# A gated delta-rule layer with a feed-forward layer on one core: the preamble shares one SBUF layout with the head units

## The reference, cut to what matters

```python
# x: (4, 1024, 256); 16 key heads, 32 value heads of 128, chunks
x = x + layernorm(attn(layernorm(x)))
x = x + layernorm(ffn(layernorm(x)))       # weights are lut[idx]; silu(gate) * up, down

def attn(x):
    mixed = silu(causal_conv4(x @ W_qkv.T))              # q, k, v
    z, b, a = x @ W_z.T, x @ W_b.T, x @ W_a.T
    beta = sigmoid(b)
    g = -exp(A_log) * softplus(a + dt_bias)              # then cumulated inside each chunk
    # per head and chunk: decay = exp(gc_i - gc_j) below the diagonal,
    # T = (I + strict(beta * k k' * decay))^-1, and a state carried from chunk to chunk
    S_new = S * exp(g_last) + (k * exp(g_last - g)).T @ v_new
    core = (q * exp(g)) @ S + ((q @ k.T) * decay) @ v_new
    return (rmsnorm(core) * norm_w * silu(z)) @ W_out.T
```

## Time and profile before

| | |
|---|---|
| median of 3 runs | 4870.68 us (4868.75 to 4873.02) |
| the profiled execution, its own time | 4866.2 us |
| its span, first to last instruction | 4864.0 us |
| PE busy in the span | 4643.0 us (95%) |
| DVE, ACT, POOL busy | 3760.0, 2864.6, 2725.4 us |
| granted TensorE clock, mean | 0.980 of full speed |

### The profile page before, as it was taken

How to read it: one execution, slowest core, us unless ns; L and a number is a source line. 1 busy time by engine, 2 the same in 40 slices (tenths; PEclk the granted TensorE clock), 3 DMA queues, 4 the chain that set the end, 5 groups by cost and what they waited for, 6 DMA issues and landing times. The chain is left out here.

```text
span 4864.0 us, 98703 instructions
## 1 busy us (share of the span) xinstructions
PE 4643.0 (95%) x33236; PEld 3450.4 (71%) x33236; DVE 3760.0 (77%) x8539; ACT 2864.6 (59%) x5549; POOL 2725.4 (56%) x8582
## 2 busy tenths in 40 slices
...
DMA packets 579249, 219.43 MB, mean 45 GB/s; under 512 B 455212, under 2 KB 541612, under 8 KB 577080
## 3 DMA queue, kind: packets, MB, share of 16 engines
...
## 5 line engine op out<-in xcount | busy, mean ns | idle before, releaser
L718 DVE SCALAR_TENSOR_TENSOR CV<-pp,CW,CV 128x1023 f32<-128x1023 f32 (+2 forms) x768 | 980.6, 1277 | 115.0 <-ACT CV L1002 108.0
L428 PE MATMUL pp<-xnT,W 128*128 128x512 f32 x2048 | 977.1, 601 | 40.6 <-DMA W<-wqkv 30.8
L1222 POOL TENSOR_TENSOR TM<-UL,XL 128x126 f32<-128x126 f32 (+22 forms) x1984 | 701.7, 354 | 277.8 <-issue 140.5
L1225 POOL TENSOR_TENSOR UL<-UL,TM 128x126 f32<-128x126 f32 (+22 forms) x1984 | 734.5, 370 | 155.4
L428 PEld LDWEIGHTS pp<-xnT,W 128*128 128x128 f32 x2048 | 375.9, 194 | 313.4 <-issue 268.3
L1086 ACT ACTIVATE QE<-qa,TAB 128x128 f32<-128x128 f32 x1024 | 319.8, 364 | 457.5 <-PE qa L553 455.8
L595 PE MATMUL emit<-Wz,xnT 128*128 128x256 f32 x2048 | 505.1, 389 | 1.0 <-DVE OACC L892 1.0
L616 PE MATMUL emit<-Wo,NTr 128*128 128x256 f32 x2048 | 497.8, 386 | 3.1 <-ACT NTr L1131 1.4
L1283 POOL TENSOR_TENSOR wd<-wd,wv 128x268 f32<-128x268 f32 x240 | 224.3, 934 | 475.3 <-DVE wv L903 475.3
L1097 ACT ACTIVATE VS<-qa,EB 128x128 f32<-128x128 f32 x1024 | 320.2, 366 | 234.6 <-PE qa L563 225.9
L827 DVE SCALAR_TENSOR_TENSOR R<-kv,TAB,V 128x128 f32<-128x128 f32 x1024 | 310.1, 344 | 182.4 <-PE kv L543 177.8
...
## 6 DMA issues: line engine op xcount, KB each, us to landing
W<-wqkv SPq DMA_DIRECT2D x256, 128.0 KB, 2.9
XL<-xb SPq DMA_DIRECT2D x128, 256.0 KB, 3.9
...
xb<-X SPq DMA_DIRECT2D x512, 32.0 KB, 1.6
...
ub<-UL SPq DMA_DIRECT2D x128, 128.0 KB, 3.0
N<-ub SPq DMA_DIRECT2D x256, 64.0 KB, 2.2
...
```

Source lines behind the costliest of these rows:

```text
L428: ins = t.matmul(bk.pp[:, 512 * h:512 * h + 512], m.W[:, c, k, :], m.xnT[:, w // KH % 2, c, 512 * h:512 * h + 512], start=c == 0, stop=c == 1)
L718: v.scalar_tensor_tensor(m.CV[:, t, d:S], bk.pp[:, 0:S - d], m.CW[:, w % KH, t, 3 - d:4 - d], m.CV[:, t, d:S], ALU.mult, ALU.add).then_inc ...
L1222: p.tensor_tensor(m.TM[:, 0:a, 0:b], m.UL[:, 0:a, k:k + 1].to_broadcast([128, a, b]), m.XL[:, k, k + 1:32].unsqueeze(1).to_broadcast([128, ...
L1225: p.tensor_tensor(m.UL[:, 0:a, k + 1:32], m.UL[:, 0:a, k + 1:32], m.TM[:, 0:a, 0:b], ALU.subtract).then_inc(s["sub"], 1)
```

## The change: what it does

1. The preamble's tensors become views of unit tiles that are not yet used (`p.X` is AT and N1, `p.xnT` is xnT and OACC, `p.tabs` are XL, Wz, Wo and half of V). The four `pre_` functions go; each engine has a `start` ahead of the only remaining barrier and a `loop` behind it.
2. `start` normalises the first 8 tiles by themselves, then the other 24. Tile 0 of unit 0 is projected between the two; the gate rows come next, with 32 weight columns for each sequence written to its own 32 PSUM partitions; then tiles 1 and 2 of unit 0, its transposes, `kred(0)`, `nk(0)` and `ldg(0)`. The normalised rows of sequences 0 and 1 stay in SBUF.
3. The pieces' DMAs of sequences 1 to 3 (six) are issued by POOL, after `nk(0)` and before the barrier.
4. `tables` (transposes into columns, Exp, negation) stands behind the barrier, and POOL issues four DMAs for them, one for each kind. Loads into XL, Wz, Wo, TAB and the copies into V (`xl`, `ldz`, `ldo`, `ldt`, `vev(0)`) wait for `tabw`, which these four DMAs raise.
5. The warm-up steps are written out once, without the parts done in `start`; from step 0 on, the loop bodies have the order of before.
6. `newton` takes three steps in place of four, everywhere.

```diff
-    for i in range(4):
+    for i in range(3):
...
-def pre_sp(nc, s, g, p, dr):
...
-def pre_dve(nc, s, g, p, bk):
...
-def pre_pe(nc, s, g, p, bk):
...
-def pre_act(nc, s, g, p, bk):
...
+def main_sp(nc, s, g, m, p, dr):
...
+    def start():
+        q.dma_start(p.X[0], dr.x.rearrange("(n p) h -> p n h", p=128)[:, 0:8, :]).then_inc(s["x0"], 16)
+        q.dma_start(g.cf[:], dr.c_f32[:, 0:129]).then_inc(s["cf"], 16)
+        ldw(0, 0)
+        ldw(0, 1)
+        q.dma_start(m.CW[:], dr.convw.rearrange("k p t j -> p k t j")).then_inc(s["cwl"], 16)
+        for j in range(1, 4):
+            q.dma_start(p.X[j], dr.x.rearrange("(n p) h -> p n h", p=128)[:, 8 * j:8 * j + 8, :]).then_inc(s[f"x{j}"], 16)
+        q.dma_start(p.wb, dr.wba).then_inc(s["wb"], 16)
+        ldw(0, 2)
+        ldw(0, 3)
+        q.dma_start(p.hd[:, 0:1], dr.dtb).then_inc(s["hd"], 16)
+        q.dma_start(p.hd[:, 1:2], dr.alog).then_inc(s["al"], 16)
+        q.dma_start(p.reset, dr.c_reset).then_inc(s["reset"], 16)
+        q.dma_start(p.last127, dr.c_f32[:, 129:257]).then_inc(s["l127"], 16)
+        q.dma_start(g.mask, dr.c_mask).then_inc(s["cb"], 16)
+        sp.wait_ge(s["ini"], 1)
+        q.dma_start(m.GR[:].bitcast(I32), dr.c_gr).then_inc(s["cbh"], 16)
+        q.dma_start(m.nw[:], dr.normw).then_inc(s["nwl"], 16)
+        q.dma_start(m.lc[:], dr.lut.to_broadcast([128, LUT])).then_inc(s["lcl"], 16)
+        for b in range(2, NB):
+            sp.wait_ge(s["xt0"], 4 * b + 4)
+            q.dma_start(dr.xnd[b], p.xnT[b]).then_inc(s["xnw"], 16)
+        for k, d in enumerate((dr.gcd, dr.gad)):
+            sp.wait_ge(s["pieces"], 5 * k + 5)
+            q.dma_start(d[:, :, 0:S], p.pieces[k][0:32]).then_inc(s["g3a"], 16)
+        for sem, n in (("cb", 16), ("cbh", 16), ("lcl", 16), ("nws", 1), ("xnw", 32)):
+            sp.wait_ge(s[sem], n)
+        ldg(0)
+    def loop():
+        ldx(0)
...
+def main_pe(nc, s, g, m, p, bk):
...
+    def start():
+        pe.wait_ge(s["cf"], 16)
+        banks = (bk.out, bk.ml, bk.mr, bk.kv)
...
+        tx(0)
+        pe.wait_ge(s["xt0"], 4)
+        for h in range(2):
+            pj(0, 0, h)
+        for b in range(1, NB):
+            tx(b)
+        pe.wait_ge(s["wb"], 16)
+        pe.wait_ge(s["xt0"], NT // 2)
+        rows = (bk.ml, bk.mr, bk.kv, bk.qa)
+        for part in range(2):
+            for half in range(2):
+                for b in range(NB):
+                    for h in range(2):
+                        ins = t.matmul(rows[2 * part + half][32 * b:32 * b + 32, :], p.wb[:, h, part, :],
+                                       p.xnT[b][:, h, 512 * half:512 * half + 512], start=h == 0, stop=h == 1)
+                ins.then_inc(s["rowp"], 1)
+        for h in range(2):
+            pj(0, 1, h)
+        for h in range(2):
+            tpq(0, h)
+        for h in range(2):
+            tpk(0, h)
+        for h in range(2):
+            pj(0, 2, h)
+    def tables():
+        banks = (bk.out, bk.ml, bk.mr, bk.kv)
+        for k, (row, ready) in enumerate(((p.ra, "gst"), (p.rb, "bst"))):
+            pe.wait_ge(s[ready], 5 if k == 0 else 3)
+            pe.wait_ge(s["rows"], 4)
+            for h in range(2):
+                pb = banks[2 * k + h]
+                for n in range(4):
+                    c = 4 * h + n
+                    ins = t.transpose(pb[:, n * 128:(n + 1) * 128], row[:, c * 128:(c + 1) * 128], g.ident)
+                ins.then_inc(s["colp"], 1)
+        pe.wait_ge(s["l127"], 16)
+        pe.wait_ge(s["col"], 2)
+        for h, pb in enumerate((bk.qa, bk.out)):
+            t.matmul(pb[:, :], p.last127, p.GC[:, 16 * h:16 * h + 16, :], start=True, stop=True).then_inc(s["glp"], 1)
+    def loop():
+        tables()
+        decp(0, 0)
+        kq(0, 0)
...
+    def start():
+        def stats(j, n0, n1):
+            for n in range(n0, n1):
+                dv.wait_ge(s[f"x{n // 8}"], 16)
+                v.bn_stats(p.st[:, n, :], p.X[n // 8][:, n % 8, :]).then_inc(s["bs"], 1)
+            for n in range(n0, n1):
+                dv.wait_ge(s["bs"], n + 1)
+                v.bn_aggr(p.mv[:, n, :], p.st[:, n, :]).then_inc(s["mv"], 1)
+            dv.wait_ge(s["mv"], n1)
+            v.tensor_scalar(p.var[:, n0:n1], p.mv[:, n0:n1, 1], 1e-5, None, ALU.add).then_inc(s["rsq"], 1)
+            newton(dv, s["rsq"], 14 * j + 1, p.var[:, n0:n1], p.rstd[:, n0:n1], p.tn[:, n0:n1])
+            dv.wait_ge(s["rsq"], 14 * j + 14)
+            for n in range(n0, n1):
+                v.tensor_scalar(p.X[n // 8][:, n % 8, :], p.X[n // 8][:, n % 8, :], p.mv[:, n, 0:1], p.rstd[:, n:n + 1],
+                                ALU.subtract, ALU.mult).then_inc(s["xn"], 1)
...
+        v.memset(m.GL[:], 1.0).then_inc(s["ini"], 1)
+        v.memset(m.VL[:], 0.0)
+        stats(0, 0, 8)
+        dv.wait_ge(s["cwl"], 16)
+        stats(1, 8, NT)
+        for d in range(1, 4):
+            cvk(0, 0, d)
+        dv.wait_ge(s["nwl"], 16)
...
+        dv.wait_ge(s["hd"], 16)
+        v.tensor_scalar(p.ra, p.ra, p.hd[:, 0:1], None, ALU.add).then_inc(s["gst"], 1)
+        dv.wait_ge(s["gst"], 1)
+        v.scalar_tensor_tensor(p.rc, p.ra, -1.0, p.ra, ALU.mult, ALU.max).then_inc(s["gst"], 1)
+        for d in range(1, 4):
+            cvk(0, 1, d)
+        dv.wait_ge(s["bexp"], 2)
+        v.scalar_tensor_tensor(p.rb, p.rb, 0.0, p.rd, ALU.min, ALU.subtract).then_inc(s["bst"], 1)
+        dv.wait_ge(s["aexp"], 2)
+        v.scalar_tensor_tensor(p.rc, p.ra, 0.0, p.rc, ALU.max, ALU.add).then_inc(s["gst"], 1)
...
+            dv.wait_ge(s["pieces"], n + 4)
+            v.tensor_copy(pc[:, 2, :], p.rc).then_inc(s["pieces"], 1)
+        kred(0)
+    def tables():
+        dv.wait_ge(s["col"], 4)
+        for h, pb in enumerate((bk.qa, bk.out)):
+            dv.wait_ge(s["glp"], h + 1)
+            v.tensor_tensor(p.DL[:, 16 * h:16 * h + 16, :], pb[:].rearrange("p (t h) -> p t h", h=32),
+                            p.BT[:, 16 * h:16 * h + 16, :], ALU.add).then_inc(s["dl"], 1)
+        dv.wait_ge(s["egt"], 4)
+        v.tensor_scalar(tab(p, NEG), tab(p, EG), -1.0, None, ALU.mult).then_inc(s["dtab"], 1)
+    def loop():
+        tables()
+        mk(0, 0)
+        x(0, 0)
...
+        if w == 0:
+            ac.wait_ge(s["tabw"], 64)
+        elif w == 1:
+            ac.wait_ge(s["g3w"], 96)
...
+        xt(0)
+        ac.wait_ge(s["cwl"], 16)
+        cv0(0, 0)
+        for b in range(1, NB):
+            xt(b)
+        ac.wait_ge(s["al"], 16)
+        a.activation(p.hd[:, 2:3], p.hd[:, 1:2], ACT.Exp).then_inc(s["ea"], 1)
+        for i, (part, row) in enumerate(((0, p.rb), (1, p.ra))):
+            for half in range(2):
+                ac.wait_ge(s["rowp"], 2 * i + half + 1)
+                a.activation(row[:, half * 512:half * 512 + 512], rows[2 * part + half][:, :],
+                             ACT.Copy).then_inc(s["rows"], 1)
+        ac.wait_ge(s["bst"], 1)
+        a.activation(p.rd, p.rd, ACT.Exp, scale=-1.0).then_inc(s["bexp"], 1)
+        cv0(0, 1)
+        ac.wait_ge(s["gst"], 2)
+        a.activation(p.rc, p.rc, ACT.Exp, scale=-1.0).then_inc(s["aexp"], 1)
+        ac.wait_ge(s["bexp"], 1)
+        a.activation(p.rd, p.rd, ACT.Ln, bias=1.0).then_inc(s["bexp"], 1)
+        ac.wait_ge(s["aexp"], 1)
+        a.activation(p.rc, p.rc, ACT.Ln, bias=1.0).then_inc(s["aexp"], 1)
+        qt(0)
+        kt(0)
+        for h in range(2):
+            qsq(0, h)
+        for h in range(2):
+            kev(0, h)
+        ksq(0)
+    def tables():
+        banks = (bk.out, bk.ml, bk.mr, bk.kv)
+        for k, col in enumerate((p.GC, p.BT)):
+            for h in range(2):
+                ac.wait_ge(s["colp"], 2 * k + h + 1)
+                a.activation(col.rearrange("p (b c) h -> p c b h", b=NB)[:, 4 * h:4 * h + 4],
+                             banks[2 * k + h][:].rearrange("p (c b h) -> p c b h", c=4, b=NB),
+                             ACT.Copy).then_inc(s["col"], 1)
+        ac.wait_ge(s["col"], 2)
+        a.activation(tab(p, EG), cols(p.GC), ACT.Exp).then_inc(s["egt"], 1)
+        for h, pb in enumerate((bk.qa, bk.out)):
+            ac.wait_ge(s["dl"], h + 1)
+            a.activation(tab(p, EGLS, h), cols(pb[:].rearrange("p (t h) -> p t h", h=32)),
+                         ACT.Exp).then_inc(s["egt"], 1)
+        a.activation(tab(p, EGLB), cols(p.DL), ACT.Exp).then_inc(s["egt"], 1)
+    def loop():
+        tables()
...
+    def start():
+        po.wait_ge(s["xtp"], NT // 2)
+        gp.memset(m.N1[0][:], 0.0)
+        gp.memset(m.N1[1][:], 0.0)
+        nk(0)
+        for k, d in enumerate((dr.gcd, dr.gad)):
+            po.wait_ge(s["pieces"], 5 * k + 5)
+            for b in range(1, NB):
+                gp.dma_start(d[:, :, b * S:b * S + S], p.pieces[k][32 * b:32 * b + 32]).then_inc(s["g3w"], 16)
+    def tables():
+        po.wait_ge(s["egt"], 4)
+        po.wait_ge(s["dtab"], 1)
+        for k in range(4):
+            gp.dma_start(dr.tabd[:, :, k].rearrange("k p t r -> p k (t r)"),
```

(69 more changed lines are left out.)

1024 lines of the change are left out of this document (499 added, 525 removed).

## The result

| | median us | runs |
|---|---|---|
| before | 4871.23 | 4868.75 to 4873.02, 4 |
| after | 4811.42 | 4805.85 to 4813.38, 4 |

The ratio of after to before is 0.9875 [0.9863, 0.9886]: the changed kernel is faster by 59.8 us, where 42.7 were forecast (4828, range 4812 to 4852). The profiled execution of after took 4813.38 us with a span of 4811.3, and 52.8 less than that of before.

What follows compares the result with a forecast made beforehand. TensorE is busy in 95% of the span, so only changes where it waits matter. The mark's 35.5 us plus 7.2 in feed-forward make 42.7; 4866.2 less that is 4823.5, with 4.5 added 4828, range 4812 to 4852.

Steps and rivals of the forecast that it cites:

- The gate rows: In the preamble, neighbouring sequences' products on separate output partitions overlap by one record: 20.8 us of rows instead of 27.7.
- rival 2: Gate rows in the preamble overlap fully, all four sequences at once: 6.9 us of rows, kernel 4814 us; chance 0.05.
- Statistics and chain: Preamble: first data at 6.7 us, eight tiles done at 15.7, all at 36.4; last piece at 83.4.
- The POOL DMAs: Six DMAs of the pieces ahead of the barrier, 0.95 us each, 5.7 in all; barrier opens at 95.8.
- Behind the barrier: Transposes, products, Exps and negation take 11.1 us to the first mask at 106.9; att of (0,3) at 126.1.
- the mark: Time at which x(0,3) of unit 0 is done: 126.1 instead of 161.65, 35.5 us earlier, moving the end alike.
- the signs that the prediction named for being wrong: vt(0) moving less than the att of (0,3), or a changed length of the stretch between unit 0 and last unit.
- Rival 3: POOL's table DMAs behind the barrier are slow, deciding from 16 us a table; 4886 us at 20; whole case 0.09.
- Rival 4: After unit 0, vt(0) doesn't follow the mark: 4838 to 4845 us; chance 0.14 together with partial cases of Rival 3.
- Feed-forward: Shorter Newton saves 0.8 us in each of nine places, eight TensorE waits and the last block's statistics: 7.2 us.
- the clock part: Feed-forward bound of 12 us if, besides, behind three waits four records no longer take 0.8 each in place of 0.43.

Runs made afterwards that it cites:

- r128: The changed kernel with gate-row weights padded to 128 output columns again, four sequences accumulated in one bank; 4830.75 us, ratio to before 0.9909.
- seq32: The changed kernel with the same 32-column gate-row products taken sequence by sequence; 4823.68 us, ratio to before 0.9899.
- b32: The kernel before with only the 32-column gate-row weights, each sequence on its own output partitions, in the old order; 4862.68 us, ratio to before 0.9988.
- r64: The changed kernel with gate-row products over 64 output columns, two sequences to each half of the output; 4820.36 us, ratio to before 0.9888.
- g3late: The changed kernel with POOL's six DMAs of the pieces moved from ahead of the barrier to behind it; 4801.97 us, ratio to before 0.9853.
- again: The changed kernel run once more, unaltered; 4810.98 us, ratio to before 0.9864.
- u0late: The changed kernel with unit 0's first work moved from the preamble's gaps to behind the tables' work; 4833.01 us, ratio to before 0.9909.

## Why the prediction was wrong, point by point

**The gate rows are the step that failed.** The prediction said that "only the last record of one can overlap the first of the next", 3 steps of 4, 20.8 us. Measured: 7.1 in after, because TensorE goes on to the next group while up to four records of the present one have still to start, not one. r128 gives the price back (27.7 us of rows, first mask 20.8 later), seq32, b32 and r64 show the rule. The rows used could not tell this: each tile there has too few records before its neighbour comes. This was rival 2, to which I gave 0.05 for "the order of the records", and its 4814 is 2.6 us from the time. The Trainium skill, TensorEngine Tiling (Array Packing), Key Properties, says that different tiles can execute weight loads and products in parallel. The runs agree in the change's order, at 3.9 times (27.7 us to 7.1); seq32 and b32 show that the order can take most of it away.

**Statistics and chain: right.** Forecast 6.7, 15.7 and 36.4 for the first data, eight tiles and all; measured 6.47, 15.3 and 35.6. From the last row copy to the last piece 24.2 us were forecast and 24.1 measured.

**The POOL DMAs: 5.7 forecast, 7.3 measured,** as two errors of opposite sign: 0.58 us an issue and not 0.95, and then 3.9 us until they had landed and the barrier opened, where the sum had some tenths. g3late and the landings show the cause. That the term came out only 1.6 us short is luck: with the issue cost right and the landing left out, it would have been 3.4.

**Behind the barrier: right, with two small errors that cancel.** The first mask at barrier + 9.4 (forecast 11.1), from there to the mark 20.3 (19.2), so the mark at + 29.8 (30.3), vt(0) 45.4 behind the mark (44.6). With the rows' 13.9 us taken off, the forecasts 95.8, 126.1 and 171 become 81.9, 112.2 and 157; measured 82.8, 112.5 and 157.9. Two of the signs that the prediction named for being wrong show by small amounts: vt(0) moved by 48.3 us and the att of (0,3) by 49.1, and the stretch from the first to the last `oacc` grew by 3.0. Both are inside what the traces of one kernel differ by (2.5 us at vt(0), 3.3 in the stretch, after against again).

**Rival 3: no.** POOL took 1.15 to 1.20 us to issue a table DMA. The four landed 14.2 us behind the first issue (92.86 to 107), 3.6 us a table where rival 3 needed 16; the forecast had 9 to 17 for all four. The starving of GpSimd's descriptors beside a two-port operation of VectorE (the Trainium skill, SBUF — State Buffer, in SBUF: two separate sides) is not seen in after, but after hardly tests it: VectorE was busy for only 2.0 of the 4.6 us of the four issues (92.86 to 97.50), with masks, x and att that take their first operand from PSUM. In u0late the three gcd DMAs were issued beside a cast on VectorE and took the same 1.82 us as in after, where VectorE stood idle. Rival 4: no, vt(0) moved with the mark (48.3 against 49.1).

**Feed-forward: the mechanism right, the term small.** 7.2 forecast, 6.4 between the two profiled executions, 8.4 on the mean of all traces; the clock part was named as a bound (up to 12 with it) and left out of the sum.

**The profiled execution.** I moved the sum by the 4.5 us between it and the median of before. That of after lies 2 us above its median, so the profiles part by 52.8 us where the times part by 59.8. The sum with 6.9 us of rows gives 56.6 and 4814; with 8.4 for the feed-forward stage 4813; the 1.5 left are inside the scatter. That it comes so close is in part luck, since the 1.6 us of the POOL DMAs and the 3.0 us by which the loop was longer in after's trace are not in this sum.
